# Moving the load of a later sequence's x behind the six copies that pack k

## The chip, the cores and the metric

The kernel runs on one core of one Trainium2 chip. The metric is the device time of one execution in microseconds (us), as a median over runs.

## The reference

One pre-layernorm decoder layer on 64 sequences of 256 tokens of width 256, in float32:

```
x = x + self_attention(layernorm(x), W, b)      # 16 heads of 16, causal, no output projection
x = x + cross_attention(layernorm(x), ctx)      # ctx: 120 rows a sequence; each token picks its best row by argmax,
                                                # and the picked rows are then the keys and values
x = x + ffn(layernorm(x))                       # each token goes to one of 4 experts (argmax), hidden width 1024,
                                                # gelu, shared output matrix, layernorm
```

## The kernel before

The kernel has two parts. The first goes over the 64 sequences: both attentions and the router, and each finished row is written to a table in HBM, sorted by expert. The second (from about 2300 us) goes over 38 tiles of up to 512 rows of that table and does the feed-forward part. Only the first part is touched.

In the first part every engine runs `for i in range(-1, B + 4)`, a software pipeline written out by hand. In step i the engines work on sequence i (maxima of the self-attention scores), i-1 (its exponentials and values), i-2, i-3 (cross-attention), i-4 (output projection, router) and prepare i+1. On TensorE, VectorE and ScalarE (ACT) a step is divided into 20 slots, numbered n; within an engine everything runs in the order in which it is written, and semaphores hold it back until what it reads is there.

The path that the change touches is that of k. For sequence i, TensorE projects k (L665). ACT makes its high part in bfloat16 (L1064, signal `k_high`), VectorE the rest (L1293), ACT the middle part (L1051, `k_mid`) and GpSimd (POOL) the low part (L1725, `k_low`). The queue of SyncE (SP) then copies these parts inside SBUF into the tile `KP`, which holds for each of 16 heads six terms side by side on the partitions: the high part three times, the middle part twice, the low part once. That is `pack` (L487): one DMA of 128 KB for each of the six terms, which wait on `k_high`, `k_mid` and `k_low` in turn. TensorE reads `KP` first in slot 8 of step i, in `self_for_max` (L709, four matmuls with the first bank of scores). Before them it waits for all six DMAs of `KP` (`k_packed`), for the same six of q (`q_packed`, issued a step earlier) and for `cmax_done`, the reading of an earlier bank of scores by VectorE (L1275).

The load of x for sequence i+2 (`load_x`, L476, 256 KB from HBM into one of two buffers `x_in`) waits for the layernorm of sequence i, which VectorE did in step i-1. It is read by `ln1_statistics` (L1242), for sequence i+2 in slot 5 of step i+1. SP's step before the change is, in this order:

```
send_self_max(i - 1)        # L520, 2 small DMAs into QP
pack k high                 # L487, 3 DMAs
load_x(i + 2)               # L476, 1 DMA
pack k middle, k low        # L487, 2 + 1 DMAs
fill_x2, load_residual, load_ctx, store_w1_piece, load_w1_piece
pack cq and send_cross_max, pack q of i + 1
```

Of the kernel before, what the change touches and what calls it, by code (L numbers as in the profile page):

```python
# [74 lines left out]
def begun(b):  # L75

    return not isinstance(b, int) or b >= 0


def decoder_kernel(nc, x, ctxT, wqkvT, bqkT, bv, wqT, wkvT, wcT, w_router, w1, b1T, wo, bo, gamma, beta, consts, out):  # L80
# [11 lines left out]
    with ExitStack() as stack:  # L92
# [342 lines left out]
        def runs(i, lag):  # L435

            return not isinstance(i, int) or 0 <= i - lag < B
# [17 lines left out]
        def _(sp):  # L455
# [15 lines left out]
            def load_x(b, par):  # L471

                if begun(b - 2):
                    sp.wait_ge(ln1_step.sem, ln1_step.value(b - 2))
                    sp.sem_inc(passed_sp, 1)
                sp.dma_start(x_in[:, par], x[bass.ds(b % B, 1)].rearrange("o (t p) c -> p (o t) c", p=P)).then_inc(x_loaded[par].sem, 16)  # L476

            def pack(b, par, terms, part, parts, ready, packed, dst, reader):

                sp.wait_ge(ready.sem, ready.value(b))  # L480
                sp.sem_inc(passed_sp, 1)
                if part == 0 and begun(b - 2):
                    sp.wait_ge(reader.sem, reader.value(b - 2))
                    sp.sem_inc(passed_sp, 1)
                for t in range(NTERM):
                    if terms[t] == part:
                        sp.dma_start(dst[D * t:D * t + D, par].rearrange("d h n -> d (h n)"), parts[:, part, :]).then_inc(packed[par].sem, 16)  # L487

            def load_residual(b, par):

                if begun(b - 2):
                    sp.wait_ge(x1_made.sem, x1_made.value(b - 2))
                    sp.sem_inc(passed_sp, 1)
                sp.dma_start(x_res[:, par], x[bass.ds(b, 1)].rearrange("o (t p) c -> p (o t) c", p=P)).then_inc(xres_loaded[par].sem, 16)

            def load_ctx(b, par):

                if begun(b - 2):
                    sp.wait_ge(match_made.sem, match_made.value(b - 2))
                    sp.sem_inc(passed_sp, 1)  # L500
                for c in range(KC):
                    sp.dma_start(ctx_sb[:, par, c, :], by_dim(ctxT[bass.ds(b, 1)].rearrange("o r m -> (o r) m"), c)).then_inc(ctx_loaded[par].sem, 16)

            def fill_x2(b, par):

                sp.wait_ge(x1_made.sem, x1_made.value(b))
                sp.sem_inc(passed_sp, 1)
                if begun(b - 2):
                    sp.wait_ge(rows_sent[par].sem, rows_sent[par].value((b - 2) // 2))
                    sp.sem_inc(passed_sp, 1)  # L510
                sp.dma_start(x2[:, par, :, 0:C], x1[:, par]).then_inc(x2_filled[par].sem, 16)

            def send_self_max(b, par):

                sp.wait_ge(mxT_copied.sem, mxT_copied.value(b))
                sp.sem_inc(passed_sp, 1)
                sp.wait_ge(q_packed[par].sem, q_packed[par].value(b // 2))
                sp.sem_inc(passed_sp, 1)
                for part in range(2):
                    sp.dma_start(QP[KR + part:KR + part + 1, par], mxT[H * part:H * part + H, :]).then_inc(mx_packed[par].sem, 16)  # L520

            def send_cross_max(b, par):

                sp.wait_ge(cmxT_copied.sem, cmxT_copied.value(b))
                sp.sem_inc(passed_sp, 1)
                for part in range(2):
                    sp.dma_start(QC[KR + 1 + part:KR + 2 + part, par], cmxT[H * part:H * part + H, :]).then_inc(cmx_packed[par].sem, 16)

            def load_w1_piece(b, par):

                if begun(b - 2):
                    sp.wait_ge(w1_piece_split.sem, w1_piece_split.value(b - 2))
                    sp.sem_inc(passed_sp, 1)
                sp.dma_start(w1_in[:, par], w1_piece(w1, b)).then_inc(w1_piece_in[par].sem, 16)

            def store_w1_piece(b, par):

                sp.wait_ge(w1_piece_split.sem, w1_piece_split.value(b))
                sp.sem_inc(passed_sp, 1)
                sp.dma_start(w1_piece(w1_high_dram, b), w1_up[:, par].bitcast(F32)).then_inc(w1_piece_out[par].sem, 16)  # L540
                sp.dma_start(w1_piece(w1_low_dram, b), w1_rest[:, par].bitcast(F32)).then_inc(w1_piece_out[par].sem, 16)

            def body(i, par):
                if runs(i, 1):
                    send_self_max(i - 1, 1 - par)
                if runs(i, 0):
                    pack(i, par, K_PARTS, 0, k_parts, k_high, k_packed, KP, st_made)
                if runs(i, -2) and begun(i):
                    load_x(i + 2, par)
                if runs(i, 0):  # L550
                    pack(i, par, K_PARTS, 1, k_parts, k_mid, k_packed, KP, st_made)
                    pack(i, par, K_PARTS, 2, k_parts, k_low, k_packed, KP, st_made)
                if runs(i, 3):
                    fill_x2(i - 3, 1 - par)
                if runs(i, 1):
                    load_residual(i - 1, 1 - par)
                    load_ctx(i - 1, 1 - par)
                    store_w1_piece(i - 1, 1 - par)
                if runs(i, 0):
                    load_w1_piece(i, par)  # L560
                if runs(i, 2):
                    pack(i - 2, par, Q_PARTS, 0, cq_parts, cq_high, cq_packed, QC, cst_made)
                if runs(i, 3):
                    send_cross_max(i - 3, 1 - par)
                if runs(i, 2):
                    pack(i - 2, par, Q_PARTS, 1, cq_parts, cq_mid, cq_packed, QC, cst_made)
                    pack(i - 2, par, Q_PARTS, 2, cq_parts, cq_low, cq_packed, QC, cst_made)
                if runs(i, -1):
                    pack(i + 1, 1 - par, Q_PARTS, 0, q_parts, q_high, q_packed, QP, st_made)
                    pack(i + 1, 1 - par, Q_PARTS, 1, q_parts, q_mid, q_packed, QP, st_made)  # L570
                    pack(i + 1, 1 - par, Q_PARTS, 2, q_parts, q_low, q_packed, QP, st_made)
                if i == 4:
                    for dst, src in late_loads:
                        sp.dma_start(dst, src).then_inc(late_weights_in, 16)
# [8 lines left out]
            for dst, src in context_loads:  # L583
                sp.dma_start(dst, src).then_inc(weights_in, 16)
            steps(sp, body)


# [1299 lines left out]
```

## Time and profile before

| | |
|---|---|
| median of 3 runs | 3206.54 us (3200.3 to 3207.85) |
| the profiled execution, its own time | 3206.65 us |
| its span, first to last instruction | 3204.7 us |
| mean granted TensorE clock | 0.983 |
| busy share of the span: TensorE (PE) | 95% |
| VectorE (DVE) | 79% |
| ScalarE (ACT) | 55% |
| GpSimd (POOL) | 39% |

The shares are means over both parts. To read what one step of the first part is worth, one looks at single steps: each takes about 35 us from the first matmul of L709 to the next step's. SPq is SP's DMA queue; an entry "x3" is three DMAs issued one behind the other, and its time is what the issuing took, not the transfer.

### The profile page before, as it was taken

To read this page: it belongs to the slowest core of one execution; us is meant where nothing else is said; L and a number is where in the kernel's file an instruction comes from. 1 tells how busy PE (TensorE), PEld (TensorE's weight loads), DVE (VectorE), ACT (ScalarE), POOL (GpSimd) and SP (SyncE) were. 2 spreads that over 40 slices of the span, in tenths; PEclk is the share of its full clock that TensorE was granted. 3 is DMA by queue.
4 is the path that set the end of the run, shared out by engine and by line. 5 is a ranking of instruction groups with operands and counts; after the bars stand their busy time and mean duration, and the time that the engine had idled before them with its cause. 6 is when DMAs were issued, how large, how long until landed. Compare 5 with 4: busy or idle time off the path is not lost.

```text
span 3204.7 us, 76256 instructions
## 1 busy us (share of the span) xinstructions
PE 3032.4 (95%) x26624; PEld 2397.4 (75%) x26624; DVE 2537.6 (79%) x6901; ACT 1753.8 (55%) x3317; POOL 1254.0 (39%) x1785
## 2 busy tenths in 40 slices
PE   5899999999999999999999999999959999999998
PEld 3667777777777777777777777777639999999998
DVE  3778888888888878888888788878748888888877
ACT  2555566556656655655665566555515445454544
POOL 3333333333333433343333333333314454544544
PEclk8999999999999999999999999999969999999999
DMA  5755565555555654565556555654324433434343
GB/s 87 118 114 105 102 114 111 103 102 114 112 101 105 113 112 99 108 115 107 99 110 118 102 99 108 119 105 94 77 78 146 142 136 128 146 123 146 129 173 131
DMA packets 323388, 364.65 MB, mean 114 GB/s; under 512 B 61886, under 2 KB 289470, under 8 KB 323008
## 3 DMA queue, kind: packets, MB, share of 16 engines
q1 hardware_dynamic: 309616, 325.63, 47.1%
q0 software_dynamic: 12576, 33.64, 3.3%
q8 instruction: 213, 3.49, 0.5%
q14 instruction: 167, 1.37, 0.2%
q10 hardware_dynamic: 816, 0.53, 0.1%
HBM read 146.45 MB, written 44.11 MB: 59 GB/s over the span
## 4 chain that ended last, share of the span: by engine, by line
PE 69%; DVE 13%; issue 8%; POOL 7%; DMA 1%; SPq 1%; ACT 1%; POOLq 0%; DVEq 0%; ACTq 0%
PE psum L665 13%; PE psum L1034 11%; PE psum L1018 10%; PE psum L660 7%; PE psum L764 4%; POOL rows_dram L1680 4%; PE psum L718 3%; PE psum L715 3%; PE psum L751 3%; PE psum L742 3%; PE psum L709 3%; DVE negmax L1270 2%; PE psum L868 2%; PE psum L748 2%; PE psum L766 2%
## 5 line engine op out<-in xcount | busy, mean ns | idle before, releaser
L1087 ACT ACTIVATE PA<-psum 128x512 f32<-128x512 f32 x512 | 306.2, 598 | 379.8 <-PE psum L751 375.8
L1270 DVE TENSOR_REDUCE negmax<-psum 128x2 f32<-128x512 f32 x512 | 344.1, 683 | 106.4 <-PE psum L718 97.2
L1206 ACT ACTIVATE hT_high<-psum,b_sb 128x512 fp32r<-128x512 f32 (+1 forms) x304 | 196.8, 647 | 400.4 <-PE psum L1018 372.8
L1093 ACT ACTIVATE PC<-psum 120x512 f32<-120x512 f32 x512 | 302.9, 594 | 175.3 <-PE psum L844 174.2
L1267 DVE TENSOR_REDUCE negmax<-psum 128x4 f32<-128x512 f32 x256 | 177.0, 691 | 195.0 <-PE psum L718 189.0
L1275 DVE TENSOR_REDUCE cnegmax<-psum 128x4 f32<-128x480 f32 x512 | 318.3, 642 | 10.9 <-PE psum L830 9.2
L1034 PE MATMUL psum<-wo_high,hT_low 128*128 128x256 f32 x1072 | 307.2, 287 | 3.5 <-DVE hT_low L1582 3.5
L1034 PE MATMUL psum<-wo_low,hT_high 128*128 128x256 f32 x1072 | 303.2, 283 | 0.0
L1034 PE MATMUL psum<-wo_high,hT_high 128*128 128x256 f32 x1072 | 303.2, 283 | 0.0
L1582 DVE TENSOR_TENSOR hT_low<-hT,hT_high 128x512 fp32r<-128x512 f32 (+1 forms) x304 | 257.1, 867 | 50.1 <-ACT hT L1207 28.7
L665 PE MATMUL psum<-zT,wqk_sb 128*128 128x256 f32 x1024 | 266.3, 383 | 3.0 <-DVE q_rest L1293 2.2
L1725 POOL TENSOR_TENSOR q_parts<-q_rest,q_parts 128x512 bf16<-128x512 f32 x64 | 74.0, 1156 | 454.4 <-ACT q_parts L1051 454.4
L751 PE MATMUL psum<-mask_t,ident_bf 128*128 128x256 bf16 (+1 forms) x768 | 239.8, 312 | 0.0
L718 PE MATMUL psum<-mask_s,ident_bf 128*128 128x256 bf16 (+1 forms) x768 | 239.3, 312 | 0.0
L1087 ACT ACTIVATE PB<-psum 128x512 f32<-128x512 f32 x256 | 152.2, 594 | 144.8 <-PE psum L751 141.4
L1018 PE MATMUL psum<-fzT_high,w_low 128*128 128x512 f32 (+1 forms) x608 | 222.6, 366 | 1.9 <-DVE fzT_low L1577 1.5
L1018 PE MATMUL psum<-fzT_low,w_high 128*128 128x512 f32 (+1 forms) x608 | 222.1, 365 | 0.0
L1018 PE MATMUL psum<-fzT_high,w_high 128*128 128x512 f32 (+1 forms) x608 | 221.9, 365 | 0.0
L665 PEld LDWEIGHTS psum<-zT,wqk_sb 128*128 128x128 f32 x1024 | 195.1, 191 | 26.7 <-DVE q_rest L1293 3.8
L742 PE MATMUL psum<-QP,KP 98*128 98x256 bf16 x1024 | 198.5, 275 | 14.1 <-DMA QP<-mxT 14.1
L1034 PEld LDWEIGHTS psum<-wo_high,hT_low 128*128 128x128 f32 x1072 | 205.5, 192 | 5.1 <-DVE hT_low L1582 5.1
L1034 PEld LDWEIGHTS psum<-wo_low,hT_high 128*128 128x128 f32 x1072 | 205.7, 192 | 0.0
(235 smaller groups left out, 8277.5 us busy)
## 6 DMA issues: line engine op xcount, KB each, us to landing
QP<-q_parts SPq DMA_DIRECT2D x384, 128.0 KB
KP<-k_parts SPq DMA_DIRECT2D x384, 128.0 KB, 4.6
QC<-cq_parts SPq DMA_DIRECT2D x384, 128.0 KB, 3.8
w_high<-w_high_dram SPq DMA_DIRECT2D x38, 1024.0 KB
w_low<-w_low_dram SPq DMA_DIRECT2D x38, 1024.0 KB
x_in<-in_x SPq DMA_DIRECT2D x64, 256.0 KB, 4.7
x_res<-in_x SPq DMA_DIRECT2D x64, 256.0 KB, 5.5
x<-x SPq DMA_DIRECT2D x64, 256.0 KB, 5.4
```

The costliest lines, as they stand in the source:

```text
L660: return pe.transpose(dst, src, identity)
L665: last = pe.matmul(psum[:, bank, m * width:(m + 1) * width], lhs(kc, m), rhs(kc), start=(kc == 0), stop=(kc == KC - 1))
L718: pe.matmul(diagonal, ident_bf[:], mask_s[:].unsqueeze(1).broadcast_to([P, masks, P]), start=False, stop=True, skip_group_check=True).then ...
L742: pe.matmul(psum[:, bank, j * T:(j + 1) * T], KP[0:KS, q, h, 0:P], QP[0:KS, q, h, :], start=(j == 0), stop=False, skip_group_check=True)
L751: pe.matmul(diagonal, ident_bf[:], mask_t[:].unsqueeze(1).broadcast_to([P, masks, P]), start=False, stop=True, skip_group_check=True).then ...
L1018: last = pe.matmul(psum[:, bank, rows], lhs, rhs, start=(n == 0), stop=(n == len(products) - 1))
L1034: last = pe.matmul(psum[:, 4 + half, j * C:(j + 1) * C], lhs, rhs, start=(m == 0 and n == 0), stop=(m == MI - 1 and n == 2))
L1087: act.activation(dst, psum[:, ST_BANKS[n % 2], :], ACT.Exp, scale=D ** -0.5).then_inc(exp_done.sem, 1)
L1093: act.activation(PC[0:M, 2 * n:2 * n + 2, :].rearrange("p h n -> p (h n)"), psum[0:M, ST_BANKS[n % 2], :], ACT.Exp, scale=D ** -0.5).then_ ...
L1270: dve.tensor_reduce(negmax[:, 1, h:h + 2], bank.rearrange("p (h k) -> p h k", h=2), AX_X, ALU.max).then_inc(max_done.sem, 1)
L1275: dve.tensor_reduce(cnegmax[:, t, 4 * g:4 * g + 4], psum[:, S_BANKS[n % 2], 0:4 * M].rearrange("p (h k) -> p h k", h=4), AX_X, ALU.max).th ...
L1582: dve.tensor_tensor(hT_low[:, m, rows], hT[:, m, rows], hT_high[:, m, rows], ALU.subtract).then_inc(h_low_made.sem, 1)
```

## The change

In each step of the first part the load of x for sequence i+2 is issued behind the three DMAs of k's middle and low parts instead of ahead of them. Its condition, its own wait, its data and its semaphore are as they were, and nothing else moves.

```diff
@@ -545,11 +545,11 @@
                     send_self_max(i - 1, 1 - par)
                 if runs(i, 0):
                     pack(i, par, K_PARTS, 0, k_parts, k_high, k_packed, KP, st_made)
-                if runs(i, -2) and begun(i):
-                    load_x(i + 2, par)
                 if runs(i, 0):
                     pack(i, par, K_PARTS, 1, k_parts, k_mid, k_packed, KP, st_made)
                     pack(i, par, K_PARTS, 2, k_parts, k_low, k_packed, KP, st_made)
+                if runs(i, -2) and begun(i):
+                    load_x(i + 2, par)
                 if runs(i, 3):
                     fill_x2(i - 3, 1 - par)
                 if runs(i, 1):
```

## Rows read from the trace of the kernel before

**Rows 1.** The page: busy time of the engines, and the granted clock in slices.
```profile
PE 3032.4 (95%) x26624; PEld 2397.4 (75%) x26624; DVE 2537.6 (79%) x6901; ACT 1753.8 (55%) x3317; POOL 1254.0 (39%) x1785
...
PEclk8999999999999999999999999999969999999999
```

**Rows 2.** Busy time by stretch: 54 steps of the first part.
```profile
core 0: us, PE busy (x) PEld busy (x) DVE busy (x) ACT busy (x) POOL busy (x), PEclk, DMA share, GB/s
235.50:2153.50 1918.00, 1857.47 (x17982) 1391.57 (x17982) 1563.57 (x4536) 1151.78 (x2214) 704.87 (x1189) 1.00 0.56 108
```

**Rows 3.** Waits in these 54 steps: us in total, times, longest.
```profile
DVE negmax L1267 <- PE psum L718: 141.0, 160, 1.8
...
DVE negmax L1270 <- PE psum L718: 83.7, 117, 0.9
...
PE psum L709 <- issue: 52.8, 51, 1.7
```

**Rows 4.** TensorE's timeline, ahead of L709 in one step: start, us, what, [idle before].
```profile
802.52 0.60 PE L660 MATMUL psum<-consts_sb,cyT 128*128 128x128 f32 x4
804.09 0.38 PE L709 MATMUL psum<-KP,QP 96*128 96x128 bf16 x4 [0.96 <-DMA KP<-k_parts]
```

**Rows 5.** The same step's last two DMAs into KP (798.0 and 798.7).
```profile
L487 SPq DMA_DIRECT2D KP<-k_parts x2: 547/570/592, 798.0 to 798.7; - x2
...
DMA to landing us min/median/max: 5.1/5.2/5.3
```

**Rows 6.** TensorE's timeline: the first L709 of nine steps, in four stretches.
```profile
235.58 0.33 PE L709 MATMUL psum<-KP,QP 96*128 96x128 bf16 x3 [1.59 <-issue]
...
1016.56 0.38 PE L709 MATMUL psum<-KP,QP 96*128 96x128 bf16 x4 [1.45 <-issue]
...
1051.65 0.38 PE L709 MATMUL psum<-KP,QP 96*128 96x128 bf16 x4 [0.64 <-issue]
...
1229.34 0.33 PE L709 MATMUL psum<-KP,QP 96*128 96x128 bf16 x3 [1.29 <-issue]
...
1263.83 0.39 PE L709 MATMUL psum<-KP,QP 96*128 96x128 bf16 x4
...
2153.55 0.33 PE L709 MATMUL psum<-KP,QP 96*128 96x128 bf16 x3 [1.04 <-issue]
...
2191.28 0.41 PE L709 MATMUL psum<-KP,QP 96*128 96x128 bf16 x2
...
2225.72 0.39 PE L709 MATMUL psum<-KP,QP 96*128 96x128 bf16 x4
...
2260.87 0.38 PE L709 MATMUL psum<-KP,QP 96*128 96x128 bf16 x4 [0.71 <-issue]
```

**Rows 7.** SP's DMA queue, timeline of the two steps that begin near 1005 and 1041.
```profile
1005.74 3.17 SPq L487 DMA_DIRECT2D KP<-k_parts  x3
1009.03 1.04 SPq L476 DMA_DIRECT2D x_in<-in_x  x1
...
1041.89 1.90 SPq L487 DMA_DIRECT2D KP<-k_parts  x3
1043.91 0.52 SPq L476 DMA_DIRECT2D x_in<-in_x  x1
1044.55 1.85 SPq L487 DMA_DIRECT2D KP<-k_parts  x3
1046.75 0.65 SPq L511 DMA_DIRECT2D x<-x  x1
```

**Rows 8.** SP's DMA queue in the two last steps, which load no x.
```profile
2216.76 3.88 SPq L487 DMA_DIRECT2D KP<-k_parts  x6
...
2251.07 5.10 SPq L487 DMA_DIRECT2D KP<-k_parts  x6
```

**Rows 9.** The last DMA into KP of the first of these two steps.
```profile
L487 SPq DMA_DIRECT2D KP<-k_parts x1: 547/547/547, 2220.1 to 2220.1; - x1
...
DMA to landing us min/median/max: 5.4/5.4/5.4
```

**Rows 10.** The load of x issued at 1043.91: its landing.
```profile
L476 SPq DMA_DIRECT2D x_in<-in_x x1: 521/521/521, 1043.9 to 1043.9; - x1
...
DMA to landing us min/median/max: 4.9/4.9/4.9
```

**Rows 11.** DMA busy tenths and GB/s, 1041 to 1052 us in 40 slices.
```profile
DMA  9410019587599959999999999999999999999999
GB/s 97 60 30 15 2 28 359 157 179 242 130 261 258 194 142 287 205 160 108 123 242 320 346 268 112 93 108 171 127 108 160 153 119 134 190 253 287 339 334 353
```

**Rows 12.** ACT's and POOL's timelines: k's middle and low part ready.
```profile
1042.59 0.63 ACT L1051 ACTIVATE k_parts<-k_rest 128x512 bf16<-128x512 f32 x1
...
1043.41 1.16 POOL L1725 TENSOR_TENSOR k_parts<-k_rest,k_parts 128x512 bf16<-128x512 f32 x1
```

**Rows 13.** VectorE's timeline around L709 and where it reads x_in.
```profile
1048.85 0.74 DVE L1242 BATCH_NORM_STATS2 stats<-x_in 128x6 f32<-128x256 f32 x2
...
1050.01 1.19 DVE L1275 TENSOR_REDUCE cnegmax<-psum 128x4 f32<-128x480 f32 x2
```

## The prediction

> **What bounds the kernel now.** I read the page first. TensorE is busy 95% of the span, VectorE 79% [rows 1]. That says which engine to follow, and not what a DMA moved in SP's queue is worth. So I took the stage that has the moved load and read it alone: in 54 steps between 235.5 and 2153.5 us TensorE is busy 1857.5 of 1918.0 us, at granted clock 1.00 (2.4 GHz) throughout [rows 2]. It idles 60.5 us. The table of waits then says where: 52.8 us of idle time stand ahead of one line, L709, in 51 of 54 steps [rows 3]. The reader is to see that nearly all of TensorE's idle time in this stage is one wait in each step, about 1 us.
>
> The table calls its releaser "issue", which means that the profile found none. In one step it did find it: at 804.09 the matmul of L709 comes after 0.96 us of idle time that a DMA into KP ended [rows 4]. The last DMA into KP of that step was issued at 798.7 and the two last took 5.1 to 5.3 us to land [rows 5]: 798.7 + 5.3 = 804.0. I take the 51 others for the same wait.
>
> Is a microsecond at this wait a microsecond of the step? The spacing of the first L709 tells. Without its idle time, TensorE reaches L709 at 1051.65 - 0.64 = 1051.01, which is 34.45 us after the previous release at 1016.56. A step that did not wait at all began 34.49 us after the one before (1263.83 after 1229.34, though that one had waited 1.29), and another 34.44 (2225.72 after 2191.28) [all rows 6]. So TensorE needs 34.45 us from one release to the next arrival, whatever the wait was, and nothing gives a wait back. The mean step is (2153.55 - 235.58) / 54 = 35.52 us [rows 6]. The difference, 1.07 us a step, is what waiting for k costs.
>
> **The change part by part.** It adds and removes no instruction. It moves one DMA of 256 KB, with its one wait, past three DMAs of 128 KB and their two waits, on SP only; POOL's queue is not passed.
>
> *Its own wait* is for a layernorm of the step before, so it costs nothing in either place.
>
> *Issue.* The x load is issued at 1043.91 and the next DMA of k at 1044.55: these three go out 0.64 us earlier [rows 7]. Their data is there: the middle part at 1042.59 + 0.63 = 1043.22, the low part at 1043.41 + 1.16 = 1044.57, while SP would come to the low part near 1045.1 (two issues of about 0.6 behind 1043.91) [rows 7, 12]. No new wait on SP in this step.
>
> *Transfer.* From 1042.6 on the DMA engines are half to wholly busy, and from 1045.1 wholly, up to 1052 [rows 11]. So what stands ahead of the last k transfer counts by its bytes, and issuing earlier while bytes stay ahead gains little. x lands at 1043.91 + 4.9 = 1048.8 [rows 7, 10], before the last k transfer, which lands by about 1051.6 when TensorE starts. Its 256 KB would take 0.9 us at 290 GB/s and 1.7 at 150; the slices have both rates [rows 11]. Below nothing is excluded, as no work is added ahead of k.
>
> *Both together* are to be read in the trace itself, because the two last steps load no x: there is no sequence 64 or 65. In the first of them six DMAs go out in 3.88 us from 2216.76, and the last, issued at 2220.1, lands 5.4 us later, at 2225.5: 8.75 us after the first issue [rows 8, 9]. With x between, in an otherwise equal step, it is 1051.6 - 1041.89 = 9.7 us [rows 6, 7]. So the value taken is 1.0 us, with 0.64 (issue only) and 0.64 + 1.7 = 2.3 (both in full) as bounds.
>
> *What becomes of 1.0 us.* The first k issue comes 1041.89 - 1016.56 = 25.33 us after the previous release [rows 6, 7]. With 8.75 that gives 34.1, earlier than TensorE's 34.45. So in an ordinary step the wait is gone and the step takes 34.45, as step 2225.72 did. But in a third of the steps (20 of 60, counted on SP's timeline) the first three issues of k take some 3.2 us in place of 1.9, as at 1005.74 [rows 7]. Steps of this kind waited longest (1.45 us at 1016.56) and took 36.0 us in the mean; the ordinary ones 35.2, over the 60 steps. The very last step is of this kind without an x load: its six issues take 5.10 us, TensorE waits 0.71 us, and the step is 2260.87 - 2225.72 = 35.15 us [rows 6, 8]. I take that as the new length of a late step.
>
> *Sum.* 40 x (35.2 - 34.45) + 20 x (36.0 - 35.15) = 30 + 17 = 47 us. The first two sequences, outside these 60, gain about 1 us each: 49. Against the profiled execution's own 3206.65 us this gives 3157.7; I say 3158. That execution is at the median of the runs, 3206.54, so the difference holds for both. Nothing is taken from the second part.
>
> *Where the moved load goes.* x will land behind k, some 3 us later than now. It is read in slot 5 of the next step: the reading at 1048.85 is of the load a step before, issued at 1009.03 [rows 7, 13], so of some 35 us of slack a tenth is used. If that cover were gone, each microsecond would stand on VectorE. The transfers behind it (x2, residual, context) keep their issue times (x2's at 1046.75, as the same commands stand before it [rows 7]) and have the same bytes ahead. What is late next is the landing of k in the late steps still, and in the others VectorE: the readings of banks (L1275) end at 1051.2, the first of the two, which TensorE needs, at about 1050.6 [rows 13], 0.4 us before TensorE arrives. Behind L709 VectorE waits for TensorE's scores, 141.0 and 83.7 us in the stage [rows 3], so it follows an earlier TensorE. DVE at 1563.6 of 1918.0 us is not the bound [rows 2].
>
> The Trainium skill (DMA: Bandwidth & Descriptors, Latency and other measured facts) puts a DMA's fixed cost at about 2 us. By that alone k's last transfer would land 2 us behind its issue and no step would wait, late ones neither; the time would be that of the second rival below. The trace speaks against it here: 5.4 us with no x ahead [rows 9]. The same page (Queues, rings and completion order) says that each DMA engine takes the descriptors of a ring in order; x landing before the last k transfer agrees.
>
> **Rivals.**
> - *Issue only* (chance 0.13). The DMA engines stay full with something else (rows being sent by POOL, instruction loads), and k gains only the 0.64 us of the issue. For: rates as low as 93 GB/s while full [rows 11]. Against: the step without x. 60 x 0.6, less what short waits can't give, is 33 us: 3173.
> - *All waits go* (0.14). The slow first issues of the late steps fall elsewhere, or their landing gains more. 60 x 1.07 = 64 us: 3142. Against: the last step still waited 0.71.
> - *No gain* (0.06). TensorE arrives earlier at L709 but another chain (the bank readings at 0.4 us behind, the GpSimd chain for rows and layernorms at the step's start) takes the wait over at nearly the old place, or the new order changes nothing as k's landing is set otherwise: 3200 to 3208. Against: arrival at 34.45 in steps with and without a wait.
> - *Slower* (0.04). The only mechanism I see with a price is the clock: in this stage it is at 1.00 all the time; its falls lie at the start and near the turn to the second part, the slice with 6 [rows 1, 2]. TensorE here gets denser, 97% to 99%. Each us at half clock (1.2 GHz) costs 0.5 us, so it takes (49 + 10) / 0.5 = 118 us of it to be slower by over 0.3%. I know no row in which denser work lowered it.
>
> **How the numbers follow.** The forecast, 3158, has 0.63, with a spread of its own of 3150 to 3167 (landing times vary by half a microsecond between equal steps). The range takes in the two rivals beside it: 3141 to 3178. About 0.3% (10 us) is what a measurement can tell from no change. Faster 0.90 (the forecast and the first two rivals), same 0.06, slower 0.04.
>
> **What would show it.** In the timeline of the changed kernel: six DMAs into KP in one entry of about 3.9 us, then x. Ordinary steps 34.4 to 34.6 us long with no idle ahead of L709, late ones about 35.1 with 0.5 to 0.7. The wait ahead of L709 falls from 53 us to 10 to 15 in the stage. x_in's readers wait for nothing. It would be wrong if steps stayed at 35 us with idle time ahead of another line (L660, L742, L830), if the six DMAs landed over 9.2 us after the first issue, or if SP met the low part unready and stood.

## The result, and the profile after

The changed kernel takes 3157.78 us (median of 5 runs, 3152.57 to 3160.29) against 3206.99 us: a ratio of 0.9853, 95% interval 0.9841 to 0.9865. Forecast were 3158 us, range 3141 to 3178. The profiled execution took 3160.29 us, its span is 3158.4 us and its mean granted clock 0.980.

Page, the line of busy time, against [rows 1]: the same work, in a span 46.3 us shorter.

```profile
PE 3032.7 (96%) x26624; PEld 2401.3 (76%) x26624; DVE 2541.0 (80%) x6901; ACT 1750.2 (55%) x3317; POOL 1262.1 (40%) x1785
```

Busy time of the same 54 steps as in [rows 2], which now lie between 230.6 and 2105.9 us:

```profile
core 0: us, PE busy (x) PEld busy (x) DVE busy (x) ACT busy (x) POOL busy (x), PEclk, DMA share, GB/s
230.60:2105.90 1875.30, 1854.78 (x17982) 1392.14 (x17982) 1563.25 (x4534) 1149.88 (x2214) 707.00 (x1189) 1.00 0.57 110
```

Waits in these 54 steps, against [rows 3]:

```profile
DVE negmax L1267 <- PE psum L718: 99.0, 133, 1.2
DVE negmax L1270 <- PE psum L718: 82.1, 110, 0.9
...
PE psum L709 <- issue: 13.5, 22, 1.1
PE psum L709 <- DVE cnegmax L1275: 0.4, 1, 0.4
```

TensorE is busy as long as before (1854.8 us against 1857.5) in 1875.3 us in place of 1918.0. The idle time ahead of L709 that the profile leaves without a releaser went from 52.8 us in 51 steps to 13.5 in 22. VectorE waits less for TensorE's scores. VectorE's readings (L1275), forecast to be next in line, ended one wait of 0.4 us.

The first L709 of seven steps in TensorE's timeline, against [rows 6]:

```profile
230.65 0.38 PE L709 MATMUL psum<-KP,QP 96*128 96x128 bf16 x4 [0.85 <-issue]
...
995.84 0.38 PE L709 MATMUL psum<-KP,QP 96*128 96x128 bf16 x4 [0.53 <-issue]
...
1030.21 0.38 PE L709 MATMUL psum<-KP,QP 96*128 96x128 bf16 x4
...
1064.50 0.39 PE L709 MATMUL psum<-KP,QP 96*128 96x128 bf16 x4
...
2105.96 0.38 PE L709 MATMUL psum<-KP,QP 96*128 96x128 bf16 x4
...
2178.01 0.39 PE L709 MATMUL psum<-KP,QP 96*128 96x128 bf16 x4
...
2213.26 0.38 PE L709 MATMUL psum<-KP,QP 96*128 96x128 bf16 x4 [0.78 <-issue]
```

The mean step is (2105.96 - 230.65) / 54 = 34.73 us, from 35.52. The step that ends at 1064.50 follows 1030.21 after 34.29 us, with no wait. The last two steps, which load no x in either kernel, are as they were: 2213.26 - 2178.01 = 35.25 us, from 35.15.

SP's queue in two steps, against [rows 7]: a late one and an ordinary one.

```profile
985.94 5.25 SPq L487 DMA_DIRECT2D KP<-k_parts  x6
991.30 0.52 SPq L476 DMA_DIRECT2D x_in<-in_x  x1
...
1021.17 3.88 SPq L487 DMA_DIRECT2D KP<-k_parts  x6
1025.16 0.52 SPq L476 DMA_DIRECT2D x_in<-in_x  x1
1026.05 0.65 SPq L511 DMA_DIRECT2D x<-x  x1
```

The last DMA into KP of the ordinary step, and its load of x, from issue to landing, against [rows 5] and [rows 10]:

```profile
L487 SPq DMA_DIRECT2D KP<-k_parts x1: 547/547/547, 1024.5 to 1024.5; - x1
...
DMA to landing us min/median/max: 5.6/5.6/5.6
...
L476 SPq DMA_DIRECT2D x_in<-in_x x1: 523/523/523, 1025.2 to 1025.2; - x1
...
DMA to landing us min/median/max: 5.5/5.5/5.5
```

k lands at 1024.5 + 5.6 = 1030.1, 8.9 us after the first issue, and L709 starts at 1030.21. x lands about 0.5 us behind k. So L709 was released by k here too, though the row above shows no idle time: the profile's modelled end of the matmul ahead covers a wait of up to 0.16 us.

DMA busy tenths and rate from 1021 to 1032 us in 40 slices, against [rows 11]:

```profile
DMA  2016769489968999999999999999999999999999
GB/s 39 2 30 224 254 145 257 123 216 295 191 123 246 268 216 115 115 186 123 119 108 142 123 115 123 149 142 119 138 168 298 331 343 350 361 342 325 331 209 283
```

The engines are as full as before. From 1025.1 to 1029.3 they carry k's copies, at 108 to 186 GB/s; then x and what follows go at 298 to 361 for 2.2 us, and at 209 and 283 in the last two slices. Only the order changed.

### The profile page after: what moved, and what is told of

Same layout as the page of the kernel before. It is cut to its first block, busy times and chain, and to the rows that moved or that the text cites. A ratio compares the mean times of both kernels' runs of the same rounds, so it can differ in the third digit from the quotient of the medians.

```text
span 3158.4 us, 76256 instructions
## 1 busy us (share of the span) xinstructions
PE 3032.7 (96%) x26624; PEld 2401.3 (76%) x26624; DVE 2541.0 (80%) x6901; ACT 1750.2 (55%) x3317; POOL 1262.1 (40%) x1785
## 4 chain that ended last, share of the span: by engine, by line
PE 70%; DVE 13%; POOL 8%; issue 7%; DMA 1%; SPq 1%; ACT 0%; POOLq 0%; DVEq 0%; ACTq 0%
PE psum L665 13%; PE psum L1034 11%; PE psum L1018 10%; PE psum L660 7%; PE psum L764 5%; POOL rows_dram L1680 4%; PE psum L718 3%; PE psum L715 3%; PE psum L751 3%; PE psum L742 3%; DVE negmax L1270 3%; PE psum L709 2%; PE psum L868 2%; PE psum L748 2%; PE psum L766 2%
## 5 line engine op out<-in xcount | busy, mean ns | idle before, releaser
L1275 DVE TENSOR_REDUCE cnegmax<-psum 128x4 f32<-128x480 f32 x512 | 318.7, 643 | 13.3 <-PE psum L830 12.7
L1680 POOL DMA_INDIRECT rows_dram<-x,row_u x128 | 134.2, 1048 | 182.4 <-issue 180.3
```

Of the source, the lines that this page charges most:

```text
L1275: dve.tensor_reduce(cnegmax[:, t, 4 * g:4 * g + 4], psum[:, S_BANKS[n % 2], 0:4 * M].rearrange("p (h k) -> p h k", h=4), AX_X, ALU.max).th ...
L1680: pool.indirect_dma_start(out=rows_dram, out_offset=bass.IndirectOffsetOnAxis(ap=row_u[:, par, t:t + 1], axis=0), in_=x2[:, par, t, :], in ...
```

## The experiments

e1 and e2 leave out most of x's bytes and so compute something else; all the others compute the whole. "Idle" is what the table of waits puts ahead of the first scores (L709, whose line number differs a little by kernel) between 235 and 2100 us, all releasers together; "step" is the mean over the same 54 steps. The kernel before, measured beside each group, took 3203.39 us (e1 to e4), 3202.45 (e5 to e8) and 3205.36 (e9 to e11), so kernels of different groups are compared by their ratios. A step is called late where SP takes over 1.0 us (1.0 to 1.9) to issue the first DMA of k, in place of 0.59, and ordinary otherwise; steps are named by their sequence.

| kernel | median us | ratio to before, interval | step us | idle us |
|---|---|---|---|---|
| before | 3206.99 | 1 | 35.52 | 52.4 |
| changed | 3157.78 | 0.9853 (0.9841 to 0.9865) | 34.73 | 13.1 |
| e1_small_old | 3156.43 | 0.9844 (0.9828 to 0.9860) | 34.70 | 12.2 |
| e2_small_new | 3155.62 | 0.9845 (0.9829 to 0.9862) | 34.71 | 12.0 |
| e3_half | 3181.28 | 0.9930 (0.9914 to 0.9947) | 35.13 | 31.2 |
| e4_between | 3209.36 | 1.0014 (1.0005 to 1.0024) | 35.62 | 56.1 |
| e5_x_late | 3156.67 | 0.9859 (0.9839 to 0.9879) | 34.71 | 13.1 |
| e6_rows_later | 3152.28 | 0.9846 (0.9827 to 0.9865) | 34.65 | 9.4 |
| e7_pad12 | 3155.36 | 0.9851 (0.9834 to 0.9867) | 34.72 | 14.0 |
| e8_pad30 | 3158.48 | 0.9861 (0.9844 to 0.9877) | 34.71 | 13.2 |
| e9_pe_pad40 | 3163.05 | 0.9870 (0.9853 to 0.9886) | 34.72 | 14.6 |
| e10_pe_pad60 | 3163.11 | 0.9871 (0.9855 to 0.9888) | 34.70 | 13.1 |
| e11_mx_on_act | 3159.90 | 0.9858 (0.9841 to 0.9874) | 34.84 | 0 |

**Issue or bytes?** The x load ahead of k's last three DMAs cost an issue of 0.64 us and 256 KB. The first pair cuts the bytes, at the old place and at the new:

```diff
+                if begun(b - 2):
+                    sp.dma_start(x_in[0:2, par], x[bass.ds(b % B, 1)].rearrange("o (t p) c -> p (o t) c", p=P)[0:2]).then_inc(x_loaded[par].sem, 16)
+                else:
+                    sp.dma_start(x_in[:, par], x[bass.ds(b % B, 1)].rearrange("o (t p) c -> p (o t) c", p=P)).then_inc(x_loaded[par].sem, 16)
-                sp.dma_start(x_in[:, par], x[bass.ds(b % B, 1)].rearrange("o (t p) c -> p (o t) c", p=P)).then_inc(x_loaded[par].sem, 16)
```

> Leaves work out: for sequences 2 to 63 the load of x brings 4 KB (two partitions) in place of 256 KB, at its old place ahead of k's middle part. The issue on SP stays, the bytes go. Theory A (the bytes ahead of k's last transfer made it late, the DMA engines being full): as fast as with the load moved, 3150 to 3163 us, ordinary steps 34.4 to 34.6 us, the first L709 without idle time in them. Theory B (the 0.64 us of the issue ahead of k's last three made it late): nothing gained, 3197 to 3210 us, steps of 35.2. A mixture would show as 3165 to 3190.

> Leaves out the same as the run before it (4 KB in place of 256 KB for sequences 2 to 63), at the new place behind k's low part. Tells what the transfer still costs where it now stands. Theory A (behind k it is free): 3158 us within 0.3%, 3149 to 3166. Rival (its 256 KB still delay somebody, x2, the residual, the context or the next parts in the queue): 5 to 20 us under 3158, more than the run before it too.

e1 on SP's queue, the load of x still between:

```profile
1052.19 2.06 SPq L490 DMA_DIRECT2D KP<-k_parts  x3
1054.37 0.38 SPq L477 DMA_DIRECT2D x_in<-in_x  x1
1054.87 1.84 SPq L490 DMA_DIRECT2D KP<-k_parts  x3
```

It has the issue at the old place (0.50 us from 1054.37 to the next of k) and the whole gain: ratio 0.9844. So x's transfer was the cause, all of it, and the issue nothing. That is theory A; B is out. The landings say the same without the kernel's time. From k's first issue to its last landing, in ordinary and in late steps, the means are 9.75 and 10.54 us before (sequences with an even number; the profile has no landing for the others), 8.81 and 9.61 in the changed kernel, and 8.79 and 9.64 in e1, whose issue of x still stands between. What isn't told apart is bytes and packets: x goes in packets of 1 KB, and e1 and e3 cut both together. e2 says what x's bytes cost at the new place: nothing that can be told (0.9845 against 0.9853, the intervals on each other).

**Half the bytes.** e3 loads one half of x at the old place and the other at the new:

```diff
+                if runs(i, -2) and begun(i):
+                    load_x(i + 2, par, (0,))
                 if runs(i, 0):
                     pack(i, par, K_PARTS, 1, k_parts, k_mid, k_packed, KP, st_made)
                     pack(i, par, K_PARTS, 2, k_parts, k_low, k_packed, KP, st_made)
                 if runs(i, -2) and begun(i):
-                    load_x(i + 2, par)
+                    load_x(i + 2, par, (1,))
```

> Nothing left out: x is loaded in two halves of 128 KB, the first at the old place and the second at the new one. Theory A (bytes): about half of the gain is lost, as k lands some 0.5 us earlier than before: 3173 to 3187 us, mean step 35.0 us. Theory B (issue): one issue still stands ahead, so the time is that of before, 3197 to 3210.

3181.28 us and a mean step of 35.13, midway between 34.73 and 35.52, as theory A had it. k lands 9.32 us (ordinary) and 10.18 us (late) behind its first issue, near the middle too. Half of the bytes, half of the cost.

**Behind which transfer?** e4 puts x between k's middle and low parts: five transfers of k ahead, one behind.

```diff
                 if runs(i, 0):
                     pack(i, par, K_PARTS, 1, k_parts, k_mid, k_packed, KP, st_made)
+                if runs(i, -2) and begun(i):
+                    load_x(i + 2, par)
+                if runs(i, 0):
                     pack(i, par, K_PARTS, 2, k_parts, k_low, k_packed, KP, st_made)
-                if runs(i, -2) and begun(i):
-                    load_x(i + 2, par)
```

> Nothing left out: the load of x stands between k's middle and low parts, so one 128 KB transfer of k is behind it and five are ahead. TensorE waits for all six. Theory A (all that counts is the bytes ahead of the last of the six): nothing gained, 3197 to 3210 us. Rival (each transfer of k that gets ahead of x gains its share): two of three gained, 3170 to 3178 us.

A step of e4, first SP's queue, then TensorE's first matmul on these scores:

```profile
1043.87 3.21 SPq L487 DMA_DIRECT2D KP<-k_parts  x5
1047.20 0.52 SPq L476 DMA_DIRECT2D x_in<-in_x  x1
1047.84 0.55 SPq L487 DMA_DIRECT2D KP<-k_parts  x1
```

```profile
1054.37 0.38 PE L710 MATMUL psum<-KP,QP 96*128 96x128 bf16 x4 [1.37 <-issue]
```

Nothing is gained: at 1.0014 of before, with an interval just above 1, it is if anything slower, and the wait is whole again (56.1 us; k lands after 9.87 and 10.54 us). Only what stands ahead of the last of the six counts.

**Later still.** e5 moves `load_x` to the step's end, just ahead of the packing of q.

> Nothing left out: the load of x stands still later, behind all transfers of the step but those of q, some 20 us later than in the changed kernel. Theory A (behind k its place is free, as it has a step of slack and the DMA engines are idle at times): 3158 us within 0.3%, 3149 to 3167. Rival (behind k it still delays x2, the residual or the context a little): 3140 to 3150. Other rival (it now delays q's transfers, which follow at once): over 3167.

0.9859: the same. x is issued 18.8 us behind k's first DMA in place of 4.2 (medians), so it moved by 14.5 us and not by the 20 that were expected. The load has room for these 14.5 us.

**What is left of the wait.** A third of the steps are still late: SP takes 1.0 to 1.9 us to issue the first DMA of k in them. Three ideas were tried on what makes it so, or what would cover it. e6 takes GpSimd's sending of rows out of the way of k:

```diff
                 if runs(i, 0):
                     make_low(i, k_mid, k_parts, k_rest, k_low)
                 if runs(i, 2):
                     root(i - 2, ln2_step, cmv, crstd, ln2_rstd, LN_EPS)
+                if runs(i, 5):
+                    send_rows(i - 1, 1 - par)
...
-                if runs(i, 4):
-                    send_rows(i, par)
```

> Nothing left out, built on the changed kernel: GpSimd sends the finished rows (264 KB by its own queue) behind k's low part and the next root of the layernorm, in the following step, in place of just ahead of them. Theory: the rows' bytes share the DMA engines with k's six transfers; without them these land up to 1 us earlier, and the late steps' remaining wait of 0.5 us ahead of L709 goes: 12.7 us in 54 steps, so 3143 to 3150 us. Rival (k's transfers are held by their own rate and by the time of issue): 3155 to 3161. Rival (SP now stands at its wait for the rows before it fills x2, and what is behind it comes late): over 3165.

By its median (3152.28 us) it came out between the theory and its first rival; by its ratio, which makes 3158 us of the 3206.99 of before, it is the first rival's. The second rival's wait is there, without a price that shows: SP now stands before it fills x2, 6.6 us behind x in place of 0.9.

```profile
1022.77 0.52 SPq L476 DMA_DIRECT2D x_in<-in_x  x1
1029.37 0.65 SPq L511 DMA_DIRECT2D x<-x  x1
```

The stage shows a little of what the theory had: 9.4 us of idle time in place of 13, a mean step of 34.65, 17 late steps in place of 22. By the time, 0.9846 against 0.9853, it can't be told from the changed kernel. It is the fastest of those that compute the whole, but not shown to be faster.

e7 and e8 put 12 and 30 idle semaphore increments ahead of SP's loop, e9 and e10 put 40 and 60 ahead of TensorE's, to shift where in the step each engine's instruction stream is refilled. e7's edit, the others are alike:

```diff
+            for _ in range(12):
+                sp.sem_inc(passed_sp, 1)
             steps(sp, body)
```

> Nothing left out: the changed kernel with 12 more semaphore increments on SP, once, ahead of the loop. Nothing waits on them. Theory F (in a third of the steps the first DMA of k is issued late because SP waits for its own instructions to be loaded, so it is their place in the program that decides): the long first issue (1.6 to 1.9 us) leaves k's first DMA and goes to commands that stand ahead of it; the time moves by up to 12 us either way, depending on where they fall. Rival G (the long issue comes from GpSimd sending rows at the same moment): k's first DMA is issued late in a third of the steps as before, the time is 3158 within 0.2%.

> As the run before it, with 30 increments in place of 12. Theory F: another place again, not k's first DMA in every third step; if all long issues then miss the six DMAs of k, ordinary steps only, 3143 to 3150 us. Rival G: as the changed kernel, 3158 within 0.2%, with the same steps late.

> Nothing left out: the changed kernel with 40 semaphore increments more on TensorE, once, ahead of the loop; nothing waits on them. In the changed kernel's trace 80 of 87 DMA issues of SP over 1.0 us long overlap one of the 16 KB loads of queue 8 (instructions), against 99 of 1524 short ones, and in the late steps such a load begins 0.1 to 0.8 us ahead of k's first DMA. Theory H (these loads are TensorE's own instructions and hold SP's issue): 40 instructions earlier in its program is some 2 us earlier in the step, so k's first DMA is no longer the long one; the long issues go to the two DMAs of mxT ahead of it or to k's last, and the count of late steps changes by more than half. The time moves by -10 to +5 us against 3158. Rival I (the loads belong to another engine, or come with SP's own issue of k): the same steps are late, 3158 within 0.2%.

> As the run before it, with 60 increments on TensorE. Theory H: the loads are some 3 us earlier in the step than in the changed kernel; those that were 0.6 us ahead of k's first DMA now fall into SP's idle time ahead of mxT and hold nothing, while others (4.8 us behind it) now fall on k's second or third DMA, which the full DMA engines cover in part: 3145 to 3158 us. Rival I: the same steps late, 3158 within 0.2%.

In all four the long issue stays on the first DMA of k (22 steps of 60 in the changed kernel, 23, 22, 22 and 21 here), and mean steps are 34.70 to 34.72. Theory F, SP's own place in its program, is out. Rival G (GpSimd sending rows at that moment) fits e7 and e8, but in e6, where the rows are sent some 5 us later, 17 such steps remain, and GpSimd sends rows in every step; so it is at most a part.

The count hides what did move: which steps are late. In the changed kernel they are nearly every third one from 22 on, with two neighbours once in 19 steps: ... 34, 37, 40, 41, 44 ... Padding SP leaves the list nearly as it was, with its pair at 40, 41 (e7, e8). Padding TensorE moves it, to 31, 32 with 40 instructions (e9) and to 25, 26 with 60 (e10). Step 29's first DMA of k, in the changed kernel and in e10:

```profile
L487 SPq DMA_DIRECT2D KP<-k_parts x1: 593/593/593, 1021.2 to 1021.2; - x1
...
L487 SPq DMA_DIRECT2D KP<-k_parts x1: 1609/1609/1609, 1026.0 to 1026.0; - x1
```

That is what TensorE's instructions would do. In the 19 steps from 30 to 49 the trace has 13053 of them, 687 a step, and 51 loads on queue 8: one load for 256 instructions. Three steps are 2061 instructions, 13 more than eight loads, so the loads come back to nearly the same place every third step and creep by 13 instructions. 40 more instructions are then 9 steps of creeping (the pair moved by 9), and 60 are 14 (it moved by 15). So theory H is right on whose loads these are, and rival I, which kept the same steps late, is wrong for e9 and e10. What H had wrong is what padding does: it changes which steps are hit and not how many. The time of e10 is outside the range that it gave.

In e9 and e10 the whole takes 3163 us. The excess lies ahead of the pipeline: TensorE's first L709 of all comes at 41.97 and 45.04 us in place of 35.57, which is 0.16 us for each added instruction.

e11 gives SP less to do ahead of k: ScalarE issues the maxima (the first hunk is SP's step, the second ScalarE's slot 0).

```diff
-                if runs(i, 1):
-                    send_self_max(i - 1, 1 - par)
...
                         add_bias(i, 1 - par, k_made, k_packed, k_parts, k_high, 7, KC)
+                    if n == 0 and runs(i, 1):
+                        send_self_max(i - 1, 1 - par)
```

> Nothing left out, built on the changed kernel: the two DMAs of the maxima (mxT, L520) are issued by ScalarE on its own queue, behind its bias of k, in place of SP just ahead of k's first. SP then comes to k's high part when it is ready, 0.8 us earlier. Theory A (what is left of the wait ahead of L709 is the landing of k in late steps, 0.5 us long): that wait goes nearly everywhere, 13 us in 54 steps: 3143 to 3150 us. Rival (ScalarE's 1.2 us of issuing in slot 0 delays its exponentials, and TensorE waits for these or for the maxima, in self_scores): the same or slower, 3156 to 3190 us.

Waits of TensorE in e11, between 235 and 2100 us, and ScalarE's timeline in one step:

```profile
PE psum L658 <- DVE V L1308: 30.0, 53, 1.5
```

```profile
1052.62 0.51 ACTq L1080 DMA_DIRECT2D QP<-mxT  x1
...
1053.16 0.61 ACTq L1080 DMA_DIRECT2D QP<-mxT  x1
1053.82 0.60 ACT L1098 ACTIVATE PC<-psum 120x512 f32<-120x512 f32 x1 [0.52 <-issue]
```

The first half of theory A came true: no idle time is left ahead of L709. SP issues k's first DMA 0.7 us earlier, and in none of 60 steps is it the long one. In steps 28, 31, 34, 37, 40, 41 and 44, late in the changed kernel, the load on queue 8 now begins 0.1 to 0.5 us behind the first issue, and the second DMA of k is the long one (1.3 to 2.0 us), here in step 28:

```profile
L487 SPq DMA_DIRECT2D KP<-k_parts x1: 1950/1950/1950, 984.6 to 984.6; - x1
```

The time did not follow: 30.0 us of idle time (2.2 in the changed kernel) now stand ahead of a transpose in slot 5 (L658), in 53 steps, where TensorE waits for VectorE's adding of v's bias (L1308), and the step is 34.84 us long, 0.11 longer. ScalarE's exponential (L1098) stands back by 0.52 us for the two issues, and what depends on it reaches TensorE late. That the delay comes by that exponential is argued from these rows, not tried. The rival was right: a wait of 13 us was traded for one of 30. The whole, 0.9858 against 0.9853, can't be told from the changed kernel.

## Why the prediction was right

*One wait a step, for k's last transfer.* Right. The profile named a releaser for it in one step of 52, and the prediction took the others for the same. The landings settle it: in each of the 27 of these 54 steps for which the trace of before has the last landing of k, L709 starts 0.09 us behind it. e1, e3 and e4 show that the landing follows the bytes ahead of the last transfer.

The Trainium skill (DMA: Bandwidth & Descriptors, Queues, rings and completion order) has each DMA engine take a ring's descriptors in order; e3 and e4 agree, with half of the cost for half of the bytes (0.9930) and all of it for five of six (1.0014).

*34.45 us from release to arrival, whatever the wait was.* Right within 0.2, and too high: the shortest steps now take 34.29. It was 34.45 with the idle time taken off because the profile's modelled end of the matmul ahead overlaps the next start by 0.16 us. So a step of before was 35.52 - 34.29 = 1.23 us longer than it could be, and not 1.07. That a wait is not given back is what made a microsecond of wait a microsecond of step.

*1.0 us for k's landing, from the two steps without x.* Right: in the mean k now lands 8.81 us behind the first issue in ordinary steps (forecast 8.75) and 9.61 in late ones, 0.94 and 0.93 us less than before. Both bounds were built from a term that is nothing: e1, which keeps 0.50 us of the 0.64 us of issue, shows it to be worth nothing here, and the transfer came out at the lower of its two prices (0.9 us at 290 GB/s; 1.7 at 150). The value taken hid no error, because it was read from whole steps and not summed from two parts.

*Ordinary 34.45, late 35.15.* Measured 34.50 and 35.09, with 22 late steps of 60 in place of 20. That ordinary steps came out at the forecast 34.45 is in part luck, as two misses cancel: TensorE could have done 34.29, and the wait in them is not gone as the prediction had it. k lands 7.7 to 9.6 us behind its first issue in them, and in 37 of the 54 steps, 22 with listed idle time and 15 without, L709 still starts 0.09 us behind k's landing. From the first L709 of sequence 1 to that of sequence 61 the time went from 2128.5 to 2083.2 us, 45.3 us, where the sum had 47. The first two sequences gave 2.3 (62.80 to 60.52 us for the L709 of sequence 1), where it had 2. Together 47.6 of the predicted 49; the second part took 1.3 us more, for no reason that I looked for, and the span is 46.3 shorter.

*Rivals.* "Issue only" is excluded by e1. "All waits go" did not happen, as the late steps stayed. "No gain" and "slower" did not: the clock was at 1.00 through the stage with TensorE at 98.9% busy.

## What to carry to other kernels

Where an engine waits for several DMAs, price what stands ahead of the last one in its queue by its bytes, and look whether the DMA engines are full there. Where they were full here, the order of issue was all that counted, and a load with a step of slack belonged behind. Look in the trace for iterations that happen to lack the thing that moves (here the two last): they are the experiment, already made. And before taking the rest of a wait by giving work to another engine, look at what that engine does in those slots: e11 removed the wait ahead of L709 and put one as costly elsewhere. And where a count stays the same after a change, look at which steps make it up.

## What the runs showed of the hardware

Two things I had not expected. The copies into KP (16 partitions each) went at 108 to 186 GB/s with all DMA engines busy, the load of x and what followed at 298 to 361 in most of the slices above: what stands ahead of a wait should be priced by its own rate. Whether it is the 16 partitions that make the copies slow was not tried.

The long issues on SP coincide with the loads of queue 8 that the page calls "instruction". Here is that queue in the changed kernel's page (before has the same 213 packets), and one long issue of the kernel before, 1.87 us for a command that else takes 0.55 to 0.6:

```profile
q8 instruction: 213, 3.49, 0.6%
```

```profile
L487 SPq DMA_DIRECT2D KP<-k_parts x1: 1865/1865/1865, 1005.7 to 1005.7; - x1
```

Counted over the changed kernel's trace between 230 and 2100 us, 80 of 87 issues over 1.0 us overlap one of these loads of 16 KB, which take 1.3 us in the median, and only 99 of 1524 shorter ones do. In the late steps around 1000 us the load begins 0.6 us ahead of k's first DMA. It is more than a coincidence: more instructions on TensorE (e9, e10) moved the loads and the long issues with them to other steps, an earlier first DMA (e11) left the long issue to the second, and more instructions on SP (e7, e8) left both in nearly the same steps. By what way a load of TensorE's instructions holds an issue of SP, no run here shows.
